# A decoder layer on one core: every engine's calls written in another sequence, and the unread products counted anew

## The reference, cut to what matters

```python
x = x + attn(layernorm(x))       # 16 heads of 32, windows of 128 rows at every 64, sigmoid scores over their row sum,
                                 # rope, K and V through a low rank and an 8-bit grid, overlapping windows blended
x = x + wkv(w, u, k=layernorm(x), v=ctx)   # a scan over 256 steps: y = (A p + E v) / (A q + E)
x = x + ffn(layernorm(x))        # bit_linear: rows rounded to 8 bits, weights to -1, 0, 1

def ffn(x):                      # x (16, 256, 512), gate and up (2048, 512), down (512, 2048)
    h = silu(bit_linear(x, w_gate)) * bit_linear(x, w_up)
    h = ln_weight * h * rsqrt(mean(h * h) + 1e-6)
    return bit_linear(h, w_down)
```

## Time and profile before

| what | us |
|---|---|
| median of 3 runs | 987.75 (984.48 to 991.34) |
| the profiled execution's own time | 982.83 |
| its span in the trace | 981.5 |
| mean granted TensorE clock | 0.991 |

### The profile page before, as it was taken

One profiled execution on the slowest core, in us unless ns is written; L12 is line 12 of the kernel. 1 busy time (PEld: TensorE's weight loads), 2 busy tenths in 40 slices (PEclk: granted clock), 3 DMA queues, 4 the chain that ended last, 5 costly groups with the idle time before them and its releaser, 6 DMA issues.

```text
span 981.5 us, 22541 instructions
## 1 busy us (share of the span) xinstructions
PE 880.1 (90%) x8575; PEld 546.3 (56%) x8674; DVE 817.0 (83%) x1520; ACT 712.5 (73%) x1188; POOL 428.2 (44%) x507
## 2 busy tenths in 40 slices
PE   6998878888898989898989899999999998987897
PEld 3456565655565656564556555556565555653453
DVE  4677688997889898998989898989797989897953
ACT  1147384667779797978788788888888878796665
POOL 2110203454454546353636463736364544545532
PEclk9999999999999999999999999999999999999999
DMA  9996360102313333323251616243333333222033
GB/s 359 393 403 224 127 224 13 61 23 62 107 45 94 87 95 86 90 87 89 78 104 65 116 65 115 68 99 82 84 63 101 74 92 79 88 75 73 14 65 97
DMA packets 119388, 107.21 MB, mean 109 GB/s; under 512 B 91792, under 2 KB 94720, under 8 KB 118128
## 3 DMA queue, kind: packets, MB, share of 16 engines
q1 hardware_dynamic: 116320, 100.64, 35.6%
q10 hardware_dynamic: 2336, 2.52, 0.8%
q0 software_dynamic: 624, 2.59, 0.7%
HBM read 65.62 MB, written 10.75 MB: 78 GB/s over the span
## 4 chain that ended last, share of the span: by engine, by line
PE 38%; DVE 20%; ACT 17%; issue 10%; DMA 5%; POOL 5%; SPq 2%; DVEq 0%; ACTq 0%; POOLq 0%
PE bank L653 10%; PE bank L673 8%; PE bank L590 7%; PE bank L582 4%; ACT arena L957 3%; DVE fs L1535 2%; ACT junk L1022 2%; PE bank L563 2%; ACT work L996 2%; PE bank L613 2%; DVE rows L1436 2%; DVE amax L1504 2%; DVE stats_wkv L1492 2%; ACT junk L1027 1%; DVE junk L1526 1%
## 5 line engine op out<-in xcount | busy, mean ns | idle before, releaser
L1858 POOL TENSOR_TENSOR work<-junk,lnw 128x512 f32<-128x512 f32 x128 | 175.2, 1387 | 182.7 <-DVE junk L1526 182.2
L653 PE MATMUL bank<-w_up_gate,qT 128*128 128x512 bf16 x967 | 227.0, 381 | 18.2 <-DMA qT<-q_tok 6.8
L653 PEld LDWEIGHTS bank<-w_up_gate,qT 128*128 128x128 bf16 x1024 | 95.2, 98 | 126.5 <-DMA qT<-q_tok 9.0
L957 ACT ACTIVATE arena<-bank 128x384 f32<-128x384 f32 x256 | 104.8, 497 | 32.6 <-PE bank L582 32.5
L673 PE MATMUL bank<-w_down,work 128*128 128x512 bf16 x470 | 112.1, 381 | 17.2 <-ACT junk L1022 6.7
L1027 ACT ACTIVATE junk<-junk,deq 128x512 f32<-128x512 f32 x128 | 92.6, 723 | 41.7 <-DVE junk L1526 41.3
L1526 DVE TENSOR_TENSOR junk<-bank,junk 128x512 f32<-128x512 f32 x128 | 85.0, 680 | 41.7 <-issue 25.0
L563 PE MATMUL bank<-wide,wq_sb 128*128 128x256 f32 x512 | 116.1, 385 | 1.3 <-DVE rows L1436 1.3
L613 PE MATMUL bank<-wo_sb,wide 128*128 128x512 f32 x256 | 113.9, 597 | 1.5 <-DVE wide L1429 1.5
L996 ACT ACTIVATE work<-work,fs 128x2048 f32<-128x2048 f32 x32 | 64.0, 2001 | 67.6 <-DVE fs L1548 67.6
L563 PEld LDWEIGHTS bank<-wide,wq_sb 128*128 128x128 f32 x512 | 97.2, 192 | 24.9 <-issue 11.8
(11 more groups left out here) (156 smaller groups left out, 1550.2 us busy)
## 6 DMA issues: line engine op xcount, KB each, us to landing
sums<-in_xT SPq DMA_DIRECT2D x8, 1024.0 KB, 9.8
wide<-in_xT SPq DMA_DIRECT2D x16, 512.0 KB, 4.6
wide<-wide SPq DMA_DIRECT2D x64, 128.0 KB, 2.1
out<-rows SPq DMA_DIRECT2D x32, 256.0 KB, 2.1
rows<-in_x SPq DMA_DIRECT2D x15, 512.0 KB, 3.6
ctx_T<-in_ctxT SPq DMA_DIRECT2D x15, 512.0 KB, 4.5
kv_b<-k_raw SPq DMA_DIRECT2D x64, 96.0 KB, 2.2
work<-in_wgT SPq DMA_DIRECT2D x4, 1024.0 KB, 13.9
```

The costliest lines, as they stand in the source:

```text
L653: last = te.matmul(bank[4 + k % 4][:, :], qT[:, c, t * P:(t + 1) * P], w_up_gate[:, m, c, cols], start=c == 0, stop=c == NC - 1)
L957: se.activation(prob[:, :, QUAD * c + j, :], bank[j][:, 0:NW * P].rearrange("p (k q) -> p k q", k=NW), ACT.Sigmoid, scale=float(1.0 / np.s ...
L1858: ge.tensor_tensor(hid_w[:, t, cols], hid[:, n % 2, :], lnw[:, cols], op=ALU.mult).then_inc(z_set.sem, 1)
```

## The change

All five lists of calls are written in another sequence. No helper changes, no buffer has another home, no wait is added or taken out, and the arithmetic that is read is the same. Only the number of unread products differs: 79 before the loop, 2 in each turn and 37 behind it become 67, 5 and 43 (140 and 170 in all). A large part of the difference in the loops is only that a turn is cut at another place: calls at its head now stand at the tail of the turn before.

The diff, cut to the places that the prediction speaks of, the loops first:

```diff
 def sync_program: the loop
-            next_keys(w)
+            next_values(f)
+            store(h, 1)
             next_queries(w)
-            turn_hidden(h, 1, 0)
-            turn_hidden(h, 1, 1)
-            store(h, 1)
             store(h, 0)
             next_residual(f)
-            next_values(f)
+            turn_tokens(f)
+            turn_hidden(g, 0, 0)
+            turn_queries(b, 0)
+            turn_hidden(g, 1, 0)
             turn_hidden(g, 0, 1)
-            turn_hidden(g, 0, 0)
-            turn_tokens(f)
-            turn_queries(b, 0)
             turn_queries(b, 1)
+            next_keys(b)
+            turn_hidden(g, 1, 1)
 def tensor_program: the loop
...
-            spin(f, 4, 2)
+            spin(f, 6, 3)
             gate_up(f, 0, 2)
             gate_up(f, 0, 3)
             scores(b, 0)
+            spin(f, 8, 2)
             down(g, 0, 0)
             scores(b, 1)
             down(g, 0, 1)
             scores(b, 2)
             down(g, 1, 0)
             scores(b, 3)
+            gate_up(f, 1, 0)
+            dens(b, 0)
+            dens(b, 1)
+            down(g, 1, 1)
...
 def scalar_program: the loop
...
             log_tables(w, 0)
+            exps(w)
             squares(f, 0, 0)
-            exps(w)
             squares(f, 0, 1)
...
 def vector_program: the loop
+            rope(w, 0)
             rope(w, 1)
             values(f)
             rotate(w, 0)
-            rotate(w, 1)
             scan(f, 0)
             scan(f, 1)
             hidden(g, 0, 2)
+            rotate(w, 1)
             hidden(g, 0, 3)
             join(f)
-            output(h, 0)
             keys_grid(b)
             peak(g, 0)
+            output(h, 0)
+            refine(f, 0)
             output(h, 1)
-            refine(f, 0)
             quotient(f, 0)
             refine(f, 1)
...
 def pool_program: before the loop
         weigh_windows(2, 1)
-        hidden_rstd(0, 0)
         weigh_windows(2, 2)
         weigh_windows(2, 3)
+        hidden_rstd(0, 0)
         weigh_hidden(0, 1, 0)
...
         weigh_hidden(1, 0, 1)
+        hidden_rstd(1, 0)
         weigh_hidden(1, 0, 2)
-        weigh_hidden(1, 0, 3)
...
 def pool_program: the loop
+            weigh_hidden(g, 0, 3)
+            first_state(w)
+            outputs(f, 0)
+            weigh_windows(w, 0)
...
             weigh_hidden(f, 0, 0)
             weigh_hidden(f, 0, 1)
-            first_state(w)
             weigh_hidden(f, 0, 2)
-            weigh_hidden(f, 0, 3)
             hidden_rstd(f, 0)
-            outputs(w, 0)
-            weigh_windows(b, 0)
...
 ahead of the loops (SP, PE, DVE) and behind them (PE, ACT)
         load_x(0)
+        load_x(1)
+        load_columns(2)
         load_small()
-        load_x(1)
         load_columns(0)
...
+        weight_total(UP)
         attention_out(0, 0)
-        weight_total(UP)
         attention_out(0, 1)
...
         attention_out(15, 1)
+        spin(13, 16, 10)
         gate_up(14, 0, 0)
...
         silu(15, 0, 0)
-        round_hidden(14, 1)
         silu(15, 0, 1)
         squares(15, 0, 0)
         silu(15, 0, 2)
         squares(15, 0, 1)
+        round_hidden(14, 1)
...
-        spin(14, 16, 23)
+        spin(14, 16, 18)
```

More of the change, by code:

```diff
@@ L800, in tensor_program @@
         scores(3, 3)
-        for i in range(4, B):
-            b, w, f, g, h = i, i - 1, i - 2, i - 3, i - 4
-            dens(w, 0)
-            dens(w, 1)
-            down(h, 1, 1)
-            dens(w, 2)
-            dens(w, 3)
-            nums(w, 0)
-            gate_up(g, 1, 0)
-            nums(w, 1)
+        dens(3, 0)
+        dens(3, 1)
+        dens(3, 2)
+        down(0, 1, 1)
+        dens(3, 3)
+        nums(3, 0)
+        gate_up(1, 1, 0)
+        nums(3, 1)
+        for i in range(4, B):
+            b, w, f, g = i, i - 1, i - 2, i - 3
             nums(w, 2)
+            nums(w, 3)
             gate_up(g, 1, 1)
-            nums(w, 3)
             gate_up(g, 1, 2)
@@ L834, in tensor_program @@
             scores(b, 3)
-        gate_up(13, 1, 0)
-        dens(15, 0)
-        dens(15, 1)
-        dens(15, 2)
-        down(12, 1, 1)
-        nums(15, 0)
-        dens(15, 3)
-        nums(15, 1)
+            gate_up(f, 1, 0)
+            dens(b, 0)
+            dens(b, 1)
+            down(g, 1, 1)
+            dens(b, 2)
+            dens(b, 3)
+            nums(b, 0)
+            nums(b, 1)
         nums(15, 2)
+        nums(15, 3)
         gate_up(13, 1, 1)
-        nums(15, 3)
         gate_up(13, 1, 2)
@@ L1093, in scalar_program @@
         silu(0, 0, 1)
+        set_keys(2)
+        silu(0, 0, 2)
         exps(1)
-        silu(0, 0, 2)
         squares(0, 0, 1)
@@ L1714, in vector_program @@
             hidden(f, 0, 1)
-            rope(b, 0)
+        rope(15, 0)
         rope(15, 1)
+        rotate(15, 0)
         values(14)
-        rotate(15, 0)
+        scan(14, 0)
         rotate(15, 1)
-        scan(14, 0)
+        scan(14, 1)
         hidden(13, 0, 2)
         hidden(13, 0, 3)
-        scan(14, 1)
         join(14)
+        output(12, 0)
         peak(13, 0)
-        output(12, 0)
-        hidden_scale(13, 0)
         refine(14, 0)
@@ L1733, in vector_program @@
         blend_windows(15, 1)
+        hidden_scale(13, 0)
+        hidden(13, 1, 0)
+        quotient(14, 1)
         blend_windows(15, 2)
-        hidden(13, 1, 0)
         hidden(13, 1, 1)
+        hidden(13, 1, 2)
         blend_windows(15, 3)
-        hidden(13, 1, 2)
-        quotient(14, 1)
         hidden(13, 1, 3)
@@ L1758, in vector_program @@
         hidden(14, 1, 0)
+        peak(14, 0)
         output(13, 0)
-        peak(14, 0)
+        refine(15, 0)
         output(13, 1)
-        refine(15, 0)
+        quotient(15, 0)
         refine(15, 1)
-        quotient(15, 0)
         quotient(15, 1)
@@ L1908, in pool_program @@
         att_rstd(0)
+        first_state(0)
         key_steps(0)
-        first_state(0)
         outputs(0, 0)
@@ L1997, in pool_program @@
         wkv_rstd(15)
+        hidden_rstd(14, 0)
         weigh_hidden(14, 1, 3)
```

415 lines of the change are left out of this document (204 added, 211 removed).

## The result

The changed kernel takes 996.94 us (median of 4 runs, 995.28 to 1002.59), the kernel before beside it 986.89 (984.48 to 991.34). The ratio is 1.0118 (1.0091 to 1.0145), so 1.2% slower and clear of the noise; slower was forecast. 1006 was forecast, so about half of the +19 came. The time lies inside the range of 989 to 1024, 1 us under the 998 to 1016 that the forecast gave itself, at the upper edge of what the prediction called "same" (978 to 998). The profiled execution is the slowest of its four: 1002.59, span 1001.3, granted clock 0.976.

A forecast was written before the change was run, and what follows sets the result against it. DVE's instruction list was taken to set the loop's turn, with PE close behind. Loop +24 (+1.8 a turn), ahead -3 and behind -2 gave +19 us on the median of 987.75, so 1006; range 989 to 1024.

The forecast's parts named there:

- hold: In each turn DVE waits at L1535 for POOL's hidden_rstd and the product behind it: 2.98 instead of 0.07 us, +2.9.
- rotate, exps: Second rotate behind the scans loses its 0.52 us idle, -0.5 a turn; exps ahead of a squares, 0, at most -0.38.
- join: DVE's four join instructions, without the fourth POOL product beside them, get shorter: -1.0 us a turn, between 0.4 and 1.7 gained.
- small steps: Second block's refine and quotient come later and meet POOL's weighings: +0.4 us a turn, between 0 and 1.9.
- Unread products: Five instead of two a turn on PE, covered by its idle time: 0; about 1 us if PE led.
- Ahead of the loop: Before the loop: later small weights +3, up weights' total -3, hidden_rstd(0, 0) -2, unread products -1; -3 us (-10 to +6).
- Behind the loop: After the loop: PE's clock kept by unread products -1.6, their excess +0.7, round_hidden -1; sum -2 us (-5 to +2).
- Rival 1: In the loop PE sets the turn and DVE's reserve takes the 2.9 us: -6.7 in twelve turns, 976 us; 7%.
- Rival 2: Join and products exclude each other, third product meets nothing, no step stretched: +0.3 to +0.9 a turn, 992 us; 17%.

The follow-up runs named there:

- the call alone: Kernel before with plain copies for the transposes, hidden_rstd(f, 0) alone moved ahead of the fourth product in the twelve turns: 1011.72 us, ratio 1.0245.
- the rotate alone: Kernel before with plain copies for the transposes, rotate(w, 1) alone moved behind the scans, between the two hidden: 1033.48 us, ratio 1.0467.
- the ground: Kernels with the two transposes made by transfers replaced by plain copies of the same bytes: 983.84 us for before, 990.23 for the changed kernel.
- without the hold: Changed kernel with plain copies, POOL's hidden_rstd of a first half moved back behind that half's fourth product: 979.47 us, ratio 0.9942 to the kernel before.

## Why the prediction was right, and where its sizes were off

The sign and the mechanism that it named were right: POOL's answer holds DVE at L1534, every turn, and the call alone makes the kernel before 2.5% slower. What a turn loses by it was mis-sized: +0.85 instead of +1.8. By its terms, for one steady turn with the transposes:

| term | forecast | measured | from |
|---|---|---|---|
| hold | +2.9 | +2.78 | 2.85 - 0.07 |
| rotate, exps | -0.5 | -0.60 | start of the join, 25.56 to 24.96 |
| join | -1.0 | -1.24 | 4.39 to 3.15 |
| small steps | +0.4 | +0.11 | quotients 1.51 to 0.99 and 1.03 to 0.68, refine 0.68 to 1.66 |
| gaps between instructions | 0 | -0.20 | the rest |
| turn | +1.8 | +0.85 | |

- *The hold* and *the rotate* came as worked out. The rotate term named SP's hidden transfers between the swaps only as harmless; by the run with the rotate alone, the moves of SP are what lets the rotate be late at all.
- *The join* was sized between two bounds and came out 0.24 better. The Trainium skill (SBUF — State Buffer, "The single rule") says that the two engines exclude each other for a whole instruction; the meetings here bear it out both ways: VectorE second takes 1.6 to 1.7 instead of 0.68 us, and GpSimd's weighing second takes 1.69 instead of 1.14.
- *The small steps* were the mis-sized idea. I counted meetings with an average price. The runs show a step function: the same instruction costs 1.66 or 0.68 us, by who is first by a few hundredths of a microsecond, and in the changed kernel all twelve turns fall on the dear side. In the long turns three steps meet a weighing, 2.3 us together on the ground, more than the 1.9 that was given as the end.
- *Unread products*: nothing, as forecast, in the loop.
- *The long turns* were missing. In the profiled execution two of them add 5.3 us, in the kernel with the call alone one adds 3.3. They start where `refine(f, 0)` loses its lead of some 0.1 us over the first weighing, and end in an idle time of PE of 2.3 us or more with the lower clock behind it. I wrote that the clock is 1.00 already; its fall comes with the last 1.0 us of such a turn.
- *Ahead of the loop*: forecast -3, in the profiled execution +7.6 (L1504 of sequence 2), in usual ones less. The 5 us later start of PE was seen; that the rest isn't caught up was not, and what keeps it stays open. *Behind the loop*: forecast -2, measured -0.1 (86.87 to 86.79). PE did keep its clock there, but the end came no earlier.

The profiled executions differ by 19.8 us: 7.6 ahead, 12.3 in the loop, -0.1 behind. The forecast for that sum was +19, and that it is so near is luck: its slow way ahead and long turns stand in for the +0.95 a turn that was forecast too much. The medians, 10.1 apart, are the fairer measure. The median lies in the range with half of the forecast change, since the range is wide.

Rival 1 (PE sets the turn) has a true core: the turn of 50.87 without the hold, with 0.93 us of new waits on DVE, shows a second limit 0.1 us under the kernel before, by the rows above ACT's inverse rather than PE. In the order of before it can't take up a hold of 2.8, as the 53.11 shows. In the changed order it nearly does: with the hold the turn is 51.12 on the ground, 0.17 over before. The sentence that nothing hides the hold was thus too strong, since without it DVE would wait or work beside POOL for most of that time. Rival 2 (+0.3 to +0.9 a turn, 992) comes as near as the forecast: +0.85 lies in its band, though by another way. The join's relief was 1.24 of its 1.68 us, and one small step is stretched where the rival had none. That DVE shows no idle up to the end of the turn, as the prediction holds against rival 1, is not so: the 0.51 us for POOL's `rstd_wkv` lie there.

## What to carry to other kernels

Before an instruction of the in-order neighbour is put ahead of a product that you wait for, price the round trip, and what it makes the next steps meet. On the ground one call moved back turned a loss of 6.4 us against before into a gain of 4.4. With the transposes that kernel was not run. An order is one object over all queues: the rotate alone cost 50 us; in the changed kernel, with SP's list moved too, the join starts 0.6 us earlier. Where two engines with short instructions on the same memory arrive within 0.05 us of each other, a forecast of that step has two values and no mean.

## What the runs showed that was not expected

- A two-operand DVE step of 0.68 us takes 1.62 to 1.69 when POOL's weighing leads by 0.03 us or more; level with it, or ahead, DVE passes, and the weighing takes 1.69 instead of 1.14. A delay of 0.2 us of DVE can so cost a turn 3.6 us.
- PE kept the full clock after idle times of 1.15 to 1.57 us in the turns with the hold. In the long ones (2.28 to 2.77) it fell to the lower of its levels, and eight transposes took 1.6 to 1.9 instead of 1.04 us. The length of the idle time alone doesn't tell: with the rotate alone the clock stayed at 1.00 around idle times of 2.73 and 2.90 us (at 315.60 and 369.32) and fell to 0.88 in the stretch around one of 2.87 (423.00).
- A plain copy of 256-byte rows lands like the transpose (2.3 against 2.4 us, 2.3 to 2.6 against 2.8 to 3.4), and SP is done with two in 1.1 to 1.35 us as a rule, instead of 2.5 or more.
